# Engine loops of a recurrent attention kernel: 15 turns over two tiles in place of 31 turns over one

## The reference

```python
def step(S, inp):
    q_t, k_t, v_t, b_g, b_beta = inp
    S = S * jnp.exp(b_g)[..., None, None]
    kv = jnp.einsum('mbhk,mbhkv->mbhv', k_t, S)
    dv = (v_t[None] - kv) * b_beta[..., None]
    S = S + k_t[..., :, None] * dv[..., None, :]
    o_t = jnp.einsum('mbhk,mbhkv->mbhv', q_t, S)
    return (S, o_t)
...
_, ys = jax.lax.scan(step, S0, (qt, kt, vt, gt, bt))
...
x = x + ga * _L0_attn_ref(h, ...)
h = _layernorm(x, axis=-1) * (1 + cb) + sb
x = x + gb * _L0_ffn_ref(h, ...)
```

## Time and profile before

| | us |
|---|---|
| time, median of 3 runs | 7274.76 (7270.02 to 7275.66) |
| time of the profiled execution | 7273.93 |
| its span, first to last instruction | 7272.2 |
| busy in it: PE, DVE, ACT, POOL | 4621.0, 5425.6, 3286.5, 2786.6 |
| mean granted TensorE clock | 0.793 |

### The profile page before, as it was taken

How to read it: one execution, slowest core, us unless ns; L and a number is a source line. 1 busy time by engine, 2 the same in 40 slices (tenths; PEclk the granted TensorE clock), 3 DMA queues, 4 the chain that set the end, 5 groups by cost and what they waited for, 6 DMA issues and landing times. The chain is left out here.

```text
span 7272.2 us, 195759 instructions
## 1 busy us (share of the span) xinstructions
PE 4621.0 (64%) x78513; PEld 3991.4 (55%) x78513; DVE 5425.6 (75%) x10088; ACT 3286.5 (45%) x5497; POOL 2786.6 (38%) x1789
## 2 busy tenths in 40 slices
PE   1666666666666666666666666666666666664994
PEld 1555555556555555555655555655565555563662
DVE  4888888888888888888888888888888888883003
ACT  1445454445444455444544445454454444541220
POOL 3444343344433434434434344343443434433003
PEclk6778877778777787777877778778787777886997
DMA  2000000000000000000000000000000000002223
GB/s 85 2 5 5 5 5 5 5 5 5 2 5 5 5 5 5 5 5 5 5 2 5 5 5 5 5 5 5 5 5 2 5 5 5 5 25 93 69 69 101
DMA packets 77478, 109.70 MB, mean 15 GB/s; under 512 B 20576, under 2 KB 66208, under 8 KB 75424
## 3 DMA queue, kind: packets, MB, share of 16 engines
q1 hardware_dynamic: 67616, 71.42, 3.1%
q0 software_dynamic: 8960, 25.39, 1.2%
HBM read 57.89 MB, written 38.89 MB: 13 GB/s over the span
## 5 line engine op out<-in xcount | busy, mean ns | idle before, releaser
L1561 POOL TENSOR_TENSOR state<-state,gc_end 128x512 f32<-128x512 f32 x512 | 594.7, 1173 | 1647.8 <-PE bank L595 1607.4
L589 PE MATMUL bank<-rhs,te 128*64 128x64 f32 x8192 | 432.2, 262 | 1054.3 <-DVE rhs L1266 725.5
L589 PEld LDWEIGHTS bank<-rhs,te 128*64 128x64 f32 x8192 | 360.4, 170 | 1141.1 <-DVE rhs L1266 1092.4
L572 PEld LDWEIGHTS bank<-state,ke 128*64 128x64 f32 x16384 | 610.5, 159 | 385.9 <-issue 194.6
L572 PE MATMUL bank<-state,ke 128*64 128x64 f32 x16384 | 649.7, 247 | 265.1 <-DVE outT L1284 171.7
L608 PE MATMUL last_two<-dvs,kte 128*64 128x64 f32 x16384 | 699.7, 250 | 179.3 <-DVE dvs L1273 179.3
L766 ACT ACTIVATE te<-tt 32x256 f32<-32x256 f32 x1024 | 421.9, 412 | 815.6 <-DVE tt L1250 805.1
L608 PEld LDWEIGHTS last_two<-dvs,kte 128*64 128x64 f32 x16384 | 637.7, 163 | 195.5 <-DVE dvs L1273 186.4
L1247 DVE TENSOR_TENSOR last_two<-last_two,prod 128x31 f32<-128x31 f32 (+15 forms) x1984 | 692.8, 349 | 68.1
L808 ACT ACTIVATE ke<-kq 32x512 f32<-32x512 f32 x1024 | 642.8, 628 | 198.6 <-DVE kq L1197 184.9
L1245 DVE TENSOR_TENSOR prod<-bd,last_two 128x31 f32<-128x31 f32 (+15 forms) x1984 | 670.6, 338 | 69.9
(11 more groups left out here) (254 smaller groups left out, 10392.7 us busy)
## 6 DMA issues: line engine op xcount, KB each, us to landing
w_sb<-in_L_ffn_W_dram SPq DMA_DIRECT2D x16, 1024.0 KB, 9.4
expert_rows<-ke SPq DMA_DIRECT2D x1, 8192.0 KB, 21.9
xrows<-expert_rows SPq DMA_DIRECT2D x16, 512.0 KB, 8.4
expert_outputs<-yrow POOLq DMA_DIRECT2D x16, 512.0 KB, 3.4
xt<-_attn_hidden_states_dram SPq DMA_DIRECT2D x32, 128.0 KB, 2.1
xr<-_attn_hidden_states_dram SPq DMA_DIRECT2D x32, 128.0 KB, 2.1
x_after_attention<-xr SPq DMA_DIRECT2D x32, 128.0 KB, 1.7
xo<-x_after_attention SPq DMA_DIRECT2D x32, 128.0 KB, 3.6
```

The lines of the kernel that those rows point to most:

```text
L572: mm = pe.matmul(bank_mem[g][s, q % 4 * DK:q % 4 * DK + DK], ke[:, c, r, q, s], state[:, hh * HQ + q, r, :], start=(r == 0), stop=(r == 1))
L589: pe.matmul(bank_mem[g][s, q % 4 * DK:q % 4 * DK + DK], te[:, q, s], rhs[:, q, :], start=True, stop=True)
L1561: pool.tensor_tensor(sv, sv, gc_end[:, vh, 4 * g:4 * g + 4, c].unsqueeze(2).broadcast_to([P, 4, 2 * DK]), ALU.mult).then_inc(sem(f"state_f ...
```

## The change

On PE, ACT, DVE and POOL the loop runs 15 turns, and its body holds two tiles, that is four halves, written out one behind the other. The tile that is left over (`half(NT - 2, 1)` and `half(NT - 1, 0)`) is written out behind the loop. The counts for each turn are doubled. The instructions of a half and their order are the same.

```diff
-        ACT_TURNS = (12, 18)
-        DVE_TURNS = (13, 26)
-        V_STEPS = (95, 190)
-        G_STEPS = (29, 26)
+        ACT_TURNS = (12, 36)
+        DVE_TURNS = (13, 52)
+        V_STEPS = (95, 380)
+        G_STEPS = (29, 52)
...
-            with dve.Fori(0, NT - 1) as n:
-                steps.enter_loop(n)
-                turns.enter_loop(n)
-                half(n, 1)
-                half(n + 1, 0)
-                steps.leave_loop(NT - 1)
-                turns.leave_loop(NT - 1)
+            with dve.Fori(0, NT // 2 - 1) as i:
+                steps.enter_loop(i)
+                turns.enter_loop(i)
+                for n in (2 * i, 2 * i + 1):
+                    half(n, 1)
+                    half(n + 1, 0)
+                steps.leave_loop(NT // 2 - 1)
+                turns.leave_loop(NT // 2 - 1)
+            half(NT - 2, 1)
+            half(NT - 1, 0)
             half(NT - 1, 1, last=True)
```

More of the change, by code:

```diff
@@ L707, in _ @@
             half(0, 0, first=True)
-            with pe.Fori(0, NT - 1) as n:
-                to_scalar.enter_loop(n)
-                to_vector.enter_loop(n)
-                half(n, 1)
-                half(n + 1, 0)
-                to_scalar.leave_loop(NT - 1)
-                to_vector.leave_loop(NT - 1)
+            with pe.Fori(0, NT // 2 - 1) as i:
+                to_scalar.enter_loop(i)
+                to_vector.enter_loop(i)
+                for n in (2 * i, 2 * i + 1):
+                    half(n, 1)
+                    half(n + 1, 0)
+                to_scalar.leave_loop(NT // 2 - 1)
+                to_vector.leave_loop(NT // 2 - 1)
+            half(NT - 2, 1)
+            half(NT - 1, 0)
             half(NT - 1, 1, last=True)
@@ L906, in _ @@
             half(0, 0, first=True)
-            with act.Fori(0, NT - 1) as n:
-                turns.enter_loop(n)
-                half(n, 1)
-                half(n + 1, 0)
-                turns.leave_loop(NT - 1)
+            with act.Fori(0, NT // 2 - 1) as i:
+                turns.enter_loop(i)
+                for n in (2 * i, 2 * i + 1):
+                    half(n, 1)
+                    half(n + 1, 0)
+                turns.leave_loop(NT // 2 - 1)
+            half(NT - 2, 1)
+            half(NT - 1, 0)
             half(NT - 1, 1, last=True)
@@ L1598, in _ @@
             half(0, 0, first=True)
[L1599 to L1603, removed]
+            with pool.Fori(0, NT // 2 - 1) as i:
+                steps.enter_loop(i)
+                for n in (2 * i, 2 * i + 1):
+                    half(n, 1)
+                    half(n + 1, 0)
+                steps.leave_loop(NT // 2 - 1)
+            half(NT - 2, 1)
+            half(NT - 1, 0)
             half(NT - 1, 1, last=True)
```

## The result

The changed kernel takes 7218.64 us (median of 6 runs, 7217.58 to 7219.99), the kernel before 7273.35 (6 runs): a ratio of 0.9925, 95% interval [0.9912, 0.9938]. It is 54.7 us faster. The forecast was 30.7 us, with 7222 as the lowest time of the range: the direction was right, the size too small by 24 us.

What follows compares the result with a forecast made beforehand. DVE's own chain, a little PE's answers, was taken to bound the kernel. 16 removed jumps at 1.84 us (29.4) plus 1.3 for the tile outside the loop gave 30.7 us, so 7244 us; range 7222 to 7260.

Steps and rivals of the forecast that it cites:

- the seam: DVE's stretch from the end of the solve (L1250) to L1147: 8.33 us with a jump, 6.06 without, 2.27 saved.
- te: ACT expands it from the solve's result; PE's corrections need it, so DVE waits 1.11 us for the second (L1273).
- PE's, ACT's and POOL's jumps are covered: Only DVE's jumps can be on the path; PE's jumps, and ACT's even at 2.7 to 3.45 us, change nothing.
- I take the middle of the measured two, 1.84: Gain per removed DVE jump, between 1.41 and 2.27 us; 16 x 1.84 = 29.4 us.
- The lower bound 1.41: Gain per jump over a whole half: 104.34 us behind a jump, 102.93 in the loop's first half without one.
- the 0.86 that the half lacked: Part of the seam's 2.27 us missing from the whole half's 1.41, put down to PE's clock in the last gram.
- one more tile outside the loop: The tile written out behind the loop saves register instructions on DVE's chain: 1.3 us, ends 0.8 and 1.7.
- a seam of 3.04: Upper bound per jump, 3.19 - 0.15 us, if PE is warm at the seam and the wait of 1.11 goes too.
- The seam gives all of it: PE's clock is high at the new seams and corrections keep up with DVE: 50.3 us, 7224; chance 0.14.
- The clock takes most back: Two PE grams a pair of tiles newly cold, leaving 9.6 us gain, 7265; chance 0.07.
- Only the branch: A jump costs only its branch of 63 ns: 1.0 us plus the tile's 1.3, so 7272; chance 0.02.
- slower: PE falls to 1.2 GHz in the grams of the new halves: 31 us slower, 7306; chance 0.02.

Runs made afterwards that it cites:

- the pair of kernels split by engine: Kernel before with only DVE's loop doubled: 7216.39 us, ratio 0.9922; with only PE's, ACT's and POOL's loops doubled: 7272.90 us, ratio 1.000.
- three kernels: Loops of 15, 6 and 2 turns (14, 5 and 1 jumps) in place of the kernel before's 30 jumps: 7218.64, 7188.17 and 7172.77 us.
- the kernel of six turns: Six turns over five tiles and one tile behind, on all four engines, against the kernel before: 7188.17 us, ratio 0.9884.
- Filler matmuls: 36 or 26 constant matmuls on PE behind its read of the memories for chunk 0, added to the kernel of six turns: 7185.60 us, ratio 0.9881.

## Why the prediction was wrong

*Right:* DVE is the pace, its jump costs 3.2 us and only at L1263, all of the gain comes from DVE's loop (shown by the pair of kernels split by engine), the seam is worth 2.27 (2.33 measured), te becomes the next late thing (PE's corrections 1.15 us late), PE's, ACT's and POOL's jumps are covered, ACT's jump becomes dear and stays hidden.

*The step that failed* is "I take the middle of the measured two, 1.84". The lower bound 1.41 was one half, the first of the loop, in which PE's clock was low during the last gram. I took this single instance for a cost that goes with a missing jump. It was no draw of the new seams at all: in the kernel before, that last gram at 1.2 GHz stands in the first half of the loop and in no other, and in the changed kernel in none of its 62 halves. What changes there is the first gram, and for the better: with 16 seams of the new kind the wait for the grams fell by 29.6 us where my sum had it rise by 0.43 x 16 = 6.9. The error in this step is 36.5 us. (The reading was rough too: of the 0.86 that the half lacked, the wait for the last gram gives 0.63 - 0.12 = 0.51; 0.27 was a wait for PE before L1223 and 0.09 one for the first gram.)

*What was left out:* POOL's instructions lengthen DVE's when they run side by side, +24.3 us. It hid most of that error: with the grams, the net of what depends on the moment is -5.3 us. That the miss was 24 us and not twice as much is luck. And the sequencer: "one more tile outside the loop" gave 1.3 us, but a second tile inside a turn also loses gaps, 9.4 us in the two lines above, which I had seen only as a property of code outside the loop. The prediction's sentence in brackets, that the two lines of 256 instructions of the Trainium skill (Advanced Engine Details and Errata, section "ISA Cache") would put ACT's doubled body outside, doesn't follow from its counts: twice 85 + 81 is 332, and 478 with the sequencer's records, both under 512. ACT's jump became dear all the same; why isn't shown.

The sum as it came out: 37.3 for the seams, 9.4 for the sequencer's gaps, 29.6 - 24.3 for grams and shared time, 4.3 for the rest, 56.3 of span. My range ended near 7222, because its largest case was a seam of 3.04 (50.3 us in all); the seam gave 2.33 on the mean, the surplus came from elsewhere in the half.

*The rivals.* "The seam gives all of it" was near in time (7224) and wrong in its mechanism: PE was as late at the new seams as at the old. "The clock takes most back" had the wrong sign. "Only the branch" and "slower" did not happen.

*What stays open.* Seam and short gaps give 2.9 us a jump in three kernels; the 11 to 14 us beside them are PE's clock, POOL's company and small lines, read off sums by line, and no run here held the clock or POOL's moments fixed to show it. Why the wait for the grams falls by nearly the same 24 to 27 us for 16, 25 and 29 jumps isn't settled, nor what the 0.36 us before L1151 are.

## What to carry over

Where a loop's body is long, look at the idle time before the first instruction of the busiest engine's turn: "issue", once per jump, is what unrolling removes, and it counts only on the engine that sets the pace. Cost it from the seam to the first instruction behind the next wait, and take the mean over many halves for everything that lies behind it, never one half. In a chain with slack of a few tenths everywhere, a microsecond added or saved at one place can come out as nothing or as two; a small probe delay costs one run and tells which. When a wait shrinks and the time doesn't, look at the same wait at the next places too: a sum over all of them hides that it moved.

## What the runs showed of the hardware that was not expected

- From branch to register instruction, ACT's jump takes 0.2 to 0.3 us with 166 recorded instructions in a turn and 2.4 to 2.9 with twice as many; DVE's takes 2.8 to 3.1 in both kernels. POOL's stays at 0.3 us in the changed kernel (4605.8 to 4606.1), with 100 recorded instructions in a turn, and takes 2.5 to 2.8 in the kernel of six turns, with 250.
- A DVE instruction of 64x128 takes 0.28, 0.94 or 1.93 us, by which POOL instruction has started before it. If POOL starts even a few hundredths of a microsecond later than DVE, it isn't lengthened.
- Filler matmuls gave PE a clock of 1.00 at the seams (mean clock of the kernel 0.862, 0.802 without), but in the even halves a low clock (0.60) then came behind PE's next pause, of 2.10 us, where the kernel without filler had 1.00 behind 1.89.
- An f32 product of two operands in SBUF took 0.36 us for 192 columns in one half and 0.90 for 210 or 1.12 for 420 in others, at a place where POOL works beside it.
- Straight code with constants in place of a loop with register values, on all engines, is worth some 1.5 us a tile of 198 (198.06 to 196.39, with one jump between the two kernels).
